# Causal masks of an attention phase: taken out of TensorE's accumulations, put into VectorE's maxima and into selects by GpSimd

## The reference

```python
x_proj = x @ Wqkv + bqkv                      # x: B, T=512, C=256
q = x_proj[:, :, :C].reshape(B, 16, T, 16)    # a plain reshape: 16 heads of width 16
k = x_proj[:, :, C:2 * C].reshape(B, 16, T, 16)
v = x_proj[:, :, 2 * C:].reshape(B, 16, T, 16)
att = einsum('bhtd,bhsd->bhts', q, k) / sqrt(16)
att = where(causal, att, -inf)
y = softmax(att) @ v                          # then back to B, T, C and through Wproj, bproj
```

## Time and profile before

| | |
|---|---|
| median of 3 runs | 4191.31 us (4186.95 to 4209.79) |
| the profiled execution, its own time | 4200.33 us |
| its span, first to last instruction | 4198.4 us |
| mean granted clock of TensorE, of full speed | 0.963 |
| PE, PEld, DVE, ACT, POOL busy, of the span | 92%, 60%, 71%, 54%, 33% |
| steady attention, 64 slots | from 1171.4 to 3522.8 us |

### The profile page before, as it was taken

The page is one execution under the profiler, slowest core; times in us unless marked ns, Lnnn a source line. Parts: engine busy times, 40 slices in busy tenths (PEclk is TensorE's granted clock), DMA queues, the critical chain, the costliest instruction groups (busy, mean ns, idle before and its releaser), DMA issues. The chain is left out here.

```text
span 4198.4 us, 81224 instructions
## 1 busy us (share of the span) xinstructions
PE 3853.1 (92%) x28814; PEld 2524.3 (60%) x28814; DVE 2985.4 (71%) x7504; ACT 2260.1 (54%) x4454; POOL 1380.0 (33%) x1724
## 2 busy tenths in 40 slices
PE   4997899997579999999999999999999996899997
PEld 4886666664345555555555555555555553667664
DVE  6997457575467777777777777777777773467575
ACT  0110466664156656666666666666666664465664
POOL 2332133332524334243333334334343320132332
PEclk8999899999689999999999999999999998899999
DMA  1332112111767677766767766777676741112111
GB/s 57 100 100 94 42 46 65 52 56 38 136 93 116 104 99 112 106 109 100 120 99 107 118 103 105 107 117 102 101 117 99 107 67 47 41 57 64 41 56 46
DMA packets 701475, 361.54 MB, mean 86 GB/s; under 512 B 305072, under 2 KB 668080, under 8 KB 701104
## 3 DMA queue, kind: packets, MB, share of 16 engines
q1 hardware_dynamic: 701104, 356.65, 47.2%
HBM read 204.49 MB, written 150.99 MB: 85 GB/s over the span
## 5 line engine op out<-in xcount | busy, mean ns | idle before, releaser
L1591 DVE TENSOR_REDUCE att_maxima<-att_s 128x1 f32<-128x512 f32 (+3 forms) x3072 | 1521.6, 549 | 434.0 <-PE att_s L1770 217.2
L1691 ACT ACTIVATE att_probs<-att_s 128x512 f32<-128x512 f32 (+1 forms) x2560 | 1330.6, 556 | 869.9 <-PE att_s L1770 511.5
L1824 PE MATMUL att_s<-att_qs,att_ks 49*128 49x512 f32 (+3 forms) x3072 | 999.2, 401 | 89.6 <-DVE att_maxima L1591 42.2
L1800 PE MATMUL att_s<-att_ks,att_qs 48*128 48x512 f32 (+3 forms) x3072 | 993.6, 408 | 20.9 <-POOL att_ks L1464 13.4
L1824 PEld LDWEIGHTS att_s<-att_qs,att_ks 49*128 49x128 f32 x3072 | 473.9, 186 | 647.5 <-ACT att_probs L1691 403.4
L1852 PE MATMUL att_o_ps<-att_probs,att_vs 128*32 128x512 f32 (+3 forms) x6144 | 632.8, 498 | 1.9 <-issue 1.1
L1770 PE MATMUL att_s<-att_mask,att_places 64*128 64x64 bf16 (+1 forms) x5632 | 590.9, 209 | 0.6 <-issue 0.6
L1800 PEld LDWEIGHTS att_s<-att_ks,att_qs 48*128 48x128 f32 x3072 | 502.3, 188 | 36.2 <-issue 16.5
L1057 PE MATMUL ffn_h2p<-ffn_h,ffn_w 128*128 128x512 f32 x768 | 366.2, 599 | 2.8 <-ACT ffn_h L938 0.7
L1770 PEld LDWEIGHTS att_s<-att_mask,att_places 64*128 64x128 bf16 x5632 | 284.1, 96 | 112.4 <-issue 43.3
L1509 POOL TENSOR_TENSOR att_x_res<-att_x_res,att_bp_row 128x512 f32<-128x512 f32 x64 | 81.3, 1283 | 748.2 <-DMA att_x_res<-x 746.7
(11 more groups left out here) (238 smaller groups left out, 5809.3 us busy)
## 6 DMA issues: line engine op xcount, KB each, us to landing
att_staged<-qk_scratch SPq DMA_DIRECT2D x768, 128.0 KB, 7.1
qk_scratch<-att_parts SPq DMA_DIRECT2D x128, 512.0 KB, 3.1
ffn_x<-x SPq DMA_DIRECT2D x64, 512.0 KB, 5.2
ssm_x<-in_L_attn_a_x_dram SPq DMA_DIRECT2D x32, 512.0 KB, 3.9
x<-ssm_y SPq DMA_DIRECT2D x32, 512.0 KB, 2.9
x<-ffn_y SPq DMA_DIRECT2D x32, 512.0 KB, 3.1
att_x<-x SPq DMA_DIRECT2D x32, 512.0 KB, 12.7
v_scratch<-att_v_tok SPq DMA_DIRECT2D x32, 512.0 KB, 3.4
```

The source lines that it names most:

```text
L1591: last = v.tensor_reduce(maxima_of[p][:, g, blk, 1 if t0 else 0:2 if t0 else 1], s1_ps[(2 * unit + 1 - g) % 3][:, col:col + w], AX.X, ALU.max)
L1691: a(probs[u % 2][2 * g + p][:, 0:n], bank[:, 0:n], ACT.Exp).then_inc(exp_done, 1)
L1800: last = mm(bank[:, col:col + w], rows_of(qs[buf], g, KROWS, p, BT * blk, BT * (blk + 1)), rows_of(ks[buf], g, KROWS, p, t0, t1), start=k ...
L1824: last = mm(bank[:, col:col + w], rows_of(ks[buf], g, SHIFT + 1, p, BT * j, BT * (j + 1)), rows_of(qs[buf], g, SHIFT + 1, p, t0, t1), star ...
```

## The change

Both masks leave PE. `masked`, `diagonals`, `places` and `mask` go, with their 5632 matmuls and weight loads, and the 20 small instructions that drew the two tiles.

The first pass's mask becomes a bf16 tile `above` of 128 x 512, which holds -1e30 above the diagonal of its last 128 columns and 0 elsewhere. Where a piece ends on the diagonal, DVE's `tensor_reduce` is replaced with a `tensor_tensor_reduce`: scores plus the last w columns of `above`, written back over the scores in PSUM, and the maximum of that into the same element of `maxima_of`. Pieces off the diagonal keep `tensor_reduce`.

The second pass's mask is applied after the exponential: `probs` becomes one tile of four heads for each set, and POOL zeroes what lies below the diagonal with one `affine_select` of 128 x 256 (both groups' heads of one p) for each diagonal piece, in `cut_probs`, after both groups' exponentials of that step. `times_v` of the units 0, 1, 2, 7, 8 and 9 waits for the new semaphore `cut`.

POOL's other tasks are cut into single instructions and spread: `lay_out`'s four pieces at 7, 8.6, 9.9 and 11.2 (before, all at 10), `normalise` at 13, 14.7, 15.7 and 16.7 (before, whole at 8), the bias of the residual at 6 (before 4). The small carrier instruction of `normalise` goes.

```diff
+    ON_DIAGONAL = [u for u, unit in enumerate(PASS2) if any(t0 == BT * j for j, t0, _ in unit)]
-    LAY_OUT_AT, PREPARE_AT, PIECES = 10, 6, 2
+    LAY_OUT_AT, PREPARE_AT, PIECES = (7, 8.6, 9.9, 11.2), 6, 2
+    BIAS_AT, NORMALISE_AT = 6, (13, 14.7, 15.7, 16.7)
-        probs = [[sb(f"probs{k}_{i}", [P, CH]) for i in range(4)] for k in range(2)]
+        above = sb("above", [P, CH], BF16)
+        probs = [sb(f"probs{k}", [P, 4, CH]) for k in range(2)]
-        places = sb("places", [P, 4, P], BF16)
-        mask = sb("mask", [P, 2, 2, GROUP], BF16)
...
+                def cut_probs(quad, step):
+
+                    u, p = step // 2, step % 2
+                    cols, col = [], 0
+                    for j, t0, t1 in PASS2[u]:
+                        if t0 == BT * j:
+                            cols.append(col)
+                        col += HD * (t1 - t0)
+                    pool.wait_ge(exp_done, 2 * STEPS * quad + 2 * step + 2)
+                    for col in cols:
+                        m = probs[u % 2][:, p::2, col:col + P]
+                        last = g.affine_select(out=m, in_=m, pattern=[[0, 2], [1, P]], compare_op=ALU.is_ge, fill=0.0,
+                                               base=0, channel_multiplier=-1)
+                    last.then_inc(cut, 1)
...
-                    tasks = []
+                    quad = 4 * b + q
+                    tasks = [(u * 2 + p + 0.5, lambda step=2 * u + p: cut_probs(quad, step))
+                             for u in ON_DIAGONAL for p in range(2)]
...
-                        tasks += [(4, lambda r=r: bias(b - 1, r)) for r in (2 * q, 2 * q + 1)]
+                        tasks += [(BIAS_AT, lambda r=2 * q + k: bias(b - 1, r)) for k in range(2)]
...
-                        tasks += [(PREPARE_AT + 2, lambda: normalise(*((2 * b + 3, 1), None, (2 * b + 4, 0))[q]))]
+                        hb, s = ((2 * b + 3, 1), None, (2 * b + 4, 0))[q]
+                        tasks += [(NORMALISE_AT[0], lambda: rstds(hb))]
+                        tasks += [(NORMALISE_AT[t], lambda t=t: normalise(hb, s, t)) for t in range(TT)]
...
-                            last = v.tensor_reduce(maxima_of[p][:, g, blk, 1 if t0 else 0:2 if t0 else 1],
-                                                   s1_ps[(2 * unit + 1 - g) % 3][:, col:col + w], AX.X, ALU.max)
+                            to = maxima_of[p][:, g, blk, 1 if t0 else 0:2 if t0 else 1]
+                            scores = s1_ps[(2 * unit + 1 - g) % 3][:, col:col + w]
+                            if t1 == BT * (blk + 1):
+                                last = v.tensor_tensor_reduce(scores, scores, above[:, CH - w:CH], 1.0, -3.0e38,
+                                                              ALU.add, ALU.max, to)
+                            else:
+                                last = v.tensor_reduce(to, scores, AX.X, ALU.max)
...
-                        if diagonals(pieces, True):
-                            last = masked(bank[:, :], 0, g, diagonals(pieces, True))
                         last.then_inc(s1_full, 1)
...
-                        if diagonals(PASS2[u], False):
-                            last = masked(bank[:, :], 1, g, diagonals(PASS2[u], False))
                         last.then_inc(s2_full, 1)
...
                     pe.wait_ge(exp_done, 2 * STEPS * quad + 4 * u + 4)
+                    if u in ON_DIAGONAL:
+                        pe.wait_ge(cut, 2 * len(ON_DIAGONAL) * quad + 2 * ON_DIAGONAL.index(u) + 2)
```

More of the change, by code:

```diff
@@ L1454, in lay_out, with normalise @@
[L1454 to L1461, removed]
-                    n = QT // PIECES
+                def normalise(hb, s, t):
+                    if t == 0:
+                        pool.wait_ge(rstd_ready, hb + 1)
+                    last = g.tensor_scalar(xt[s][:, t, :], xt[s][:, t, :], moments[:, t, 0:1], rstd[:, t:t + 1],
+                                           ALU.subtract, ALU.mult)
+                    if t == TT - 1:
+                        last.then_inc(xn_ready, 1)
@@ L1463, in lay_out, with lay_out_all @@
+                def lay_out_all(quad, side):
                     for e in range(PIECES):
-                        last = g.tensor_copy(
-                            stack[0:ROWS, :].rearrange("p (t c) -> p t c", c=HD)[:, e * n:(e + 1) * n, :],
-                            staged[side][0:ROWS, :, e * n:(e + 1) * n].rearrange("p c t -> p t c"))
-                    last.then_inc(laid_out[side], 1)
+                        lay_out(quad, side, e, False)
                 def make_masks():
-                    for m in (places[:, :, :], mask[:, :, :, :]):
-                        g.memset(m, 0.0).then_inc(mask_zero, 1)
+                    g.memset(above[:, :], 0.0).then_inc(above_ready, 1)
+                    pool.wait_ge(above_ready, 1)
+                    m = above[:, CH - P:CH]
+                    g.affine_select(out=m, in_=m, pattern=[[-1, P]], compare_op=ALU.is_ge, fill=-1e30, base=0,
+                                    channel_multiplier=1).then_inc(above_ready, 1)
@@ L1690, in exponentiate @@
                     bank = s2_ps[s2_use(q, step, g) % 3]
[L1691 removed]
+                    a(probs[u % 2][:, 2 * g + p, 0:n], bank[:, 0:n], ACT.Exp).then_inc(exp_done, 1)
                 def project(hb, j, index):
@@ L1801, in first_piece @@
                               rows_of(ks[buf], g, KROWS, p, t0, t1), start=k == 0,
-                              stop=k == len(pieces) - 1 and not diagonals(pieces, True))
+                              stop=k == len(pieces) - 1)
                     if k == len(pieces) - 1:
-                        if diagonals(pieces, True):
-                            last = masked(bank[:, :], 0, g, diagonals(pieces, True))
                         last.then_inc(s1_full, 1)
```

88 lines of the change are left out of this document (31 added, 57 removed).

## The result

The kernel after takes 4217.43 us (median of 20 runs, 4192.75 to 4248.68), the kernel before 4197.0 (20 runs). The ratio is 1.005, 95% interval 1.0029 to 1.0071: slower by half a per cent, where 4157 and faster was forecast (0.30 was given to slower and 0.17 to a change within 0.5%, at whose edge the measured 20 us lie; the range reached to 4310).

The account below looks back on a forecast made before the run. PE and DVE were taken to bound the first halves, PE alone the second. First halves 68.6 to 68.5, second 79.5 - 7.0 + 5.0 = 77.5: -2.1 us a batch row, times 16 = -34, giving 4157 us; 8-in-10 range 4050 to 4310.

Parts of the forecast that it names:

- granted clock still about 1: PE in the attention: its clock stays near full after the change, as the 0.99 read before it.
- DVE's piece: Each fused diagonal piece on DVE takes 0.10 us more than the plain reduction, between 0.07 and 0.13.
- the 0.05 that the prediction named as a sign of being wrong: Prediction is wrong if DVE's fused pieces cost under 0.05 or over 0.15 us more than reductions.
- The forecast's 6.4 us for the first halves: DVE's added time for the 64 fused pieces in a batch row's first halves (steps 0 to 9).
- My 0.07 as the least that it adds: DVE's tiny second instruction, writing out the maximum, adds at least 0.07 us a piece; saving then 64 us.
- some 100: Saving in us by the prediction's sum if DVE's fused form costs nothing extra.
- Change 0: First halves (steps 0 to 9): DVE needs 68.5 us against 68.6 now, so PE's 7.0 saved become waiting.
- the ceiling: PE's masks cost some 0.04 us each: 14.1 us in a batch row, 225 in all, the most to gain.
- there PE alone sets the pace: Second halves (steps 10 to 19): DVE hidden under PE; 79.5 - 7.0 for masks + 5.0 for POOL = 77.5 us.
- POOL: the mechanism: times_v waits for POOL's late selects, stalling PE by 5.0 us a batch row in the second halves.
- cheap and hidden: Rival 1, 25%: fused form costs 0.03 us or less, POOL's cuts mostly in time; -138 us, 4053.
- rivals 2 and 3: 2: DVE becomes the bound (20%), +120 us at 0.25 a piece, 4311. 3: POOL becomes it (12%), +160, 4350.

Follow-up runs that it names:

- 14: Kernel before, every mask on PE, with PE's first three groups of steps 18 and 19 in every slot waiting for ACT's group just before; 4694 us.
- 15: Kernel before without the second pass's masks (left out of the computation), plus waits of PE for ACT in steps 18 and 19 of every slot; 4416 us.
- 10: Kernel after, but PE masks the second pass's units 7, 8 and 9 and POOL selects only in units 0, 1 and 2; 4135 us.
- 11: Kernel after, but PE masks the second pass's units 0, 1 and 2 and POOL selects only in units 7, 8 and 9; 4304 us.
- run 5: Kernel after with the second pass's masks added by PE as well, POOL's selects and DVE's fused pieces kept; 4196 us.
- Runs 6: Kernel before without any first-pass mask, maxima taken over whole rows by plain reductions, second pass's masks on PE; 4101 us.
- 9: Kernel before without the second pass's masks, which are left out of the computation with nothing in their place; 4155 us.
- run 8: Kernel after without POOL's selects and the wait for them, so the second mask is left out; POOL's new order stays; 4169 us.
- run 2: Kernel after with the first pass's masks back on PE and plain reductions on DVE; POOL still selects for the second pass; 4302 us.

## Why the prediction was wrong

**The step that failed: "granted clock still about 1".** It was point (a) of what the profile would show, and every term of the sum took it for granted. After's runs have 581 us at half clock on average, before's 294: 287 x 0.32 = 92 us that the sum did not have. At the clock of before, after would take 4123, a gain of 76 instead of the loss of 17 (mean spans 4215.8 and 4198.8). That added idle time alone can do it, runs 14 and 15 show; that the places of masks and selects matter and not their number alone, runs 10 and 11 show; that masks on PE help at nearly the same idle time, run 5 shows. The 92 us rest on the slope within kernels, a correlation. After's own batch rows, carried to no half clock, give 142.6 us against 148.1: a gain of 88, and a loss to the clock of 105 (0.40 for each of the 262 us that the attention has more). Run 10, with half of the selects and the clock up, bears it out: 142.4 us a row, and 4135.

**DVE's piece: over-sized.** 0.10 us was taken, between 0.07 and 0.13, from four tiny instructions in a row. Between independent instructions the accumulator's read hides: 0.036 to 0.050 of busy time, 0.011 to 0.016 of the kernel's time at full clock, under the 0.05 that the prediction named as a sign of being wrong. DVE's busy time of the batch row is 120.3 us, not 129. The forecast's 6.4 us for the first halves became 1.4 to 2.1 in the whole batch row. PE's waits for its maxima did not grow from 2.7 to 7 us in the batch row; they were 2.9:

```profile
PE att_s L1822 <- ACT att_probs L1712: 3.1, 7, 0.7
PE att_s L1822 <- DVE att_maxima L1612: 1.6, 2, 0.8
PE att_s L1822 <- DVE att_maxima L1609: 1.3, 3, 1.0
...
PE att_o_ps L1850 <- POOL att_probs L1506: 1.1, 1, 1.1
```

The Trainium skill (VectorE: DVE Perf Modes, § Two Vector instructions with no wait between them) had the two instructions right: the trace shows DVE_READ_ACCUMULATOR2_ANT, 2048 times at 141 ns. My 0.07 as the least that it adds was not the page's, and was wrong. So was the side sum beside it: with nothing added, the prediction's own sum gives 8.5 us a row or 136, not "some 100".

**"Change 0" in the first halves: wrong.** The 68.4 us hold a stretch at half clock. Run 10, with the same work on DVE, has 65.8 at full clock, where before has 68.6 and the forecast 68.5. DVE did not eat PE's 7.0 us there; 2.8 came through, or 45 us in 16 batch rows. That 68.4 was measured is luck.

**PE's masks: the ceiling was right, the split was not.** Runs 6 and 9 take each pass's masks away: at full clock a batch row falls from 148.1 to 141.7 and 144.4. At 0.04 us each, the 160 masks of the first pass are 6.4 us, and all of it came. The 192 of the second are 7.7, and 3.7 came: 2.3 of 3.8 in the first halves, and in the second halves, of which the forecast said "there PE alone sets the pace" (from a half slot's mean, 77.0 of 79.5 us busy), 1.5 of 3.8. PE waits for ACT instead: between 1300 and 3300 us its waits for exponentials are 39.1 us in run 9, where before has 18.2, and those for maxima 26.8 instead of 35.4:

```profile
PE att_s L1824 <- ACT att_probs L1691: 39.1, 81, 0.8
PE att_s L1824 <- DVE att_maxima L1591: 26.8, 54, 0.9
```

**POOL: the mechanism right, the size half.** Selects at 408 ns (0.45 forecast). PE's idle time in steps 16 to 19, after against run 8, is 1.1 us more in q = 2 (1.8 forecast), 0.3 in q = 0 (2.6), and the same in q = 1 and 3 (0.7 each). Measured 2.6 us a batch row with PE's masks in place and 1.6 without (8 against after; 1.3 by the rows), not 5.0. But what they cost by the clock came on top: run 2 against run 9 is 147 us, and the rows at full clock differ by 1.9, or 30 of them.

**The rivals.** At equal clock the truth (-76, or -88 by the rows) lies between the forecast (-34) and "cheap and hidden" (-138). The loss came by none of the named ways: rivals 2 and 3 gave too little gain for engines' work, and the measured loss is PE's clock. For the one batch row shown the sum looks right, 146.0 forecast and 146.3 measured; that is luck, because a stretch at half clock took what the small pieces gave.

## What to carry to other kernels

Matmuls that look superfluous may keep TensorE's clock up: before taking work off an engine that is 96% busy, find where it will stand idle afterwards, and put a price on the clock there, here 0.3 to 0.4 us for each us at half clock. Work is best taken from the stretches where that engine sets the pace, and left where it waits for others anyway (run 10 against run 11: 169 us for the same instructions, nearly all of it the clock's). And a mean over half a slot hides the steps in which the bound changes; cut the windows by steps where the removed instructions stand. A sum that agrees with a window says little until the window's clock is read beside it.

## What the runs showed of the hardware

TensorE's clock fell after idle time made of short gaps: in run 14 none in the window above is over 0.7 us, PE is busy for 8.57 of 10.20 us, and 14.38 us follow at 0.53. Before has 6.81 of 7.37 busy in the same steps and keeps its clock. But run 14's slot with q = 3, with 8.18 of 10.38 us busy, keeps it too, so these numbers alone do not foretell a single dip. The Trainium skill (TensorE: Matmul & The Clock Gate, § A second HAM failure mode: psum-queue depth-cycling) tells of a kernel whose clock went up and down for small idle times between groups of matmuls; these traces agree, and show it with gaps of at most 0.7 us.

The last thing not expected: runs of the same kernel differ by their half-clock time. After's 20 runs span 4190.9 to 4246.8 us at clocks of 0.942 to 0.923, while before's stay within 0.959 to 0.971. The kernel whose clock falls is also the less steady one.
